# Layer 0 attention: the product of probabilities and values for two query tiles at once, in two-part reduced-precision operands

## The reference, cut to what matters

```
q = (h @ dequant(qw_q)).heads   # 32 heads; 4-bit weights with a scale per 128 rows
k, v = the same with 8 heads    # each serves 4 query heads (REP0 = 4)
q, k = rope(q), rope(k)
scores = q @ k.T / sqrt(128), causal
attn = softmax(scores)
ctx = attn @ v                  # <- the product that is changed
x = x + gate * (ctx @ dequant(qw_o))
```

## Time and profile before

| | |
|---|---|
| median of three runs | 1750.33 us |
| the profiled execution's own time | 1747.66 us |
| its span, first to last instruction | 1745.8 us |
| mean granted TensorE clock | 0.978 of 2.4 GHz |
| busy: PE, DVE, ACT, POOL | 1654.7, 1170.5, 1044.1, 747.5 us |
| first and last weight load of the changed product (L778) | 74.1 and 967.1 us |
| from an output product of head 0 to the same one of head 30 | 102.6 to 939.8 us, 30 heads |

### The profile page before, as it was taken

How to read it: one execution, slowest core, us unless ns; L and a number is a source line. 1 busy time by engine, 2 the same in 40 slices (tenths; PEclk the granted TensorE clock), 3 DMA queues, 4 the chain that set the end, 5 groups by cost and what they waited for, 6 DMA issues and landing times. The chain is left out here.

```text
span 1745.8 us, 28527 instructions
## 1 busy us (share of the span) xinstructions
PE 1654.7 (95%) x10107; PEld 1337.1 (77%) x10123; DVE 1170.5 (67%) x2951; ACT 1044.1 (60%) x2261; POOL 747.5 (43%) x705
## 2 busy tenths in 40 slices
PE   4899999999999999999999799999988999999897
PEld 2699989999999989899988488878764555555476
DVE  5767677777777676777666743336777777776285
ACT  3477777877777777777777221114324666666553
POOL 3286585675856757567551300000352334321200
PEclk9999999999999999999999889999979999999998
DMA  6100000101010010000000512200230000000000
GB/s 195 38 14 24 26 25 20 31 13 38 13 31 25 19 37 13 25 19 25 13 19 7 166 46 70 68 1 19 84 83 13 1 1 1 1 1 1 1 19 31
DMA packets 75014, 55.82 MB, mean 32 GB/s; under 512 B 23502, under 2 KB 57998, under 8 KB 74874
## 3 DMA queue, kind: packets, MB, share of 16 engines
q1 hardware_dynamic: 73290, 53.21, 10.5%
q10 hardware_dynamic: 1584, 0.79, 0.2%
HBM read 51.88 MB, written 2.10 MB: 31 GB/s over the span
## 5 line engine op out<-in xcount | busy, mean ns | idle before, releaser
L778 PEld LDWEIGHTS psum<-a_probsT,a_v 128*128 128x128 f32 x2304 | 294.7, 191 | 25.6 <-issue 3.9
L778 PE MATMUL psum<-a_probsT,a_v 128*128 128x128 f32 x2304 | 299.2, 275 | 1.7 <-ACT a_probsT L988 1.6
L877 DVE CUSTOM_DVE_ANT_0 psum<-psum,a_keys_allowed 128x128 f32<-128x128 f32 (+7 forms) x256 | 195.7, 764 | 83.1 <-PE psum L78 74.5
L2109 ACT ACTIVATE a_probsT<-psum 128x512 f32<-128x512 f32 (+1 forms) x304 | 168.4, 588 | 106.1 <-PE psum L1976 67.4
L971 ACT ACTIVATE a_probs<-psum,a_neg_max 128x128 f32<-128x128 f32 (+7 forms) x256 | 190.7, 745 | 66.4 <-DVE a_neg_max L877 58.0
L980 ACT ACTIVATE a_probs<-a_probs,a_row_inv 128x128 f32<-128x128 f32 (+7 forms) x256 | 201.2, 786 | 27.8 <-DVE a_row_inv L884 27.6
L641 POOL TENSOR_TENSOR a_turned_pool<-a_q_sum,a_sine 64x512 f32<-64x512 f32 x62 | 79.3, 1279 | 286.8 <-DVE a_q_sum L863 285.6
L907 DVE TENSOR_TENSOR a_ctxT_lo<-psum,a_ctxT_hi 128x128 fp32r<-128x128 f32 x256 | 73.5, 287 | 172.7 <-ACT a_ctxT_hi L994 172.6
L988 ACT COPY a_probsT<-psum 128x512 f32<-128x512 f32 (+3 forms) x384 | 173.3, 488 | 18.8 <-PE psum L766 16.6
L897 DVE SCALAR_TENSOR_TENSOR a_sumT<-psum,a_scale_o,a_sumT 128x512 f32<-128x512 f32 x248 | 173.5, 741 | 0.9 <-PE psum L792 0.8
L766 PE MATMUL psum<-ident,a_probs 128*128 128x128 f32 x1152 | 168.9, 274 | 0.5 <-ACT a_vT L965 0.3
(11 more groups left out here) (394 smaller groups left out, 3891.3 us busy)
## 6 DMA issues: line engine op xcount, KB each, us to landing
a_raw_o<-in_L_attn_qw_o SPq DMA_DIRECT2D x32, 256.0 KB, 2.8
a_raw_q<-in_L_attn_qw_q SPq DMA_DIRECT2D x31, 256.0 KB, 3.6
mod1b_w<-in_L_wmod SPq DMA_DIRECT2D x4, 1024.0 KB, 6.2
mod0a_w<-in_L_wmod SPq DMA_DIRECT2D x3, 1024.0 KB, 12.8
mod0b_w<-in_L_wmod SPq DMA_DIRECT2D x3, 1024.0 KB, 7.5
f_raw<-in_L_ffn_down_w SPq DMA_DIRECT2D x10, 256.0 KB, 3.1
f_raw<-in_L_ffn_gate_w SPq DMA_DIRECT2D x10, 256.0 KB, 3.3
f_raw<-in_L_ffn_up_w SPq DMA_DIRECT2D x10, 256.0 KB, 3.6
```

Of the source, the lines that this page charges most:

```text
L778: last = nc.tensor.matmul(bank(use)[:, 0:P], v[:, g % 2, j, :], probsT[:, u % 2, j, :], start=(j == 0), stop=(j == i))
L877: nc.vector.tensor_tensor_reduce(out=scores, in0=scores, in1=keys_allowed[:, S - (i + 1) * P:S], scale=-1.0, scalar=-MASKED, op0=ALU.add, ...
L2109: nc.scalar.activation(probsT[:, s % SLOTS, hs[0]:hs[-1] + 1, first:HALF], scores_of(group, n, HALF - first), ACT.Exp).then_inc(exped.sem, 1)
```

## The change

The product of probabilities and v is done once for two query tiles (2m and 2m + 1 of a head) with 256 columns, and with both operands in two f32r parts: three products for each of the 2m + 1 key tiles that both query tiles see. The last key tile, which only the odd query tile sees, keeps one float32 product with 128 columns (`own`). `values` for the pair stands in every odd iteration, at the place where one of a single unit stood in every iteration.

The operands have to be made: ACT copies the turned probabilities to `probsT_hi` (and the last key tile of an odd unit to `own` by a copy of its own), and DVE, new, computes `probsT_lo` from the bank and `probsT_hi` (`low_probs`) at the end of its iteration. The bank of turned probabilities is free only after DVE's part, not after ACT's. The values get the same parts (`high_v` on ACT, two instructions in `take_v` on DVE), at iterations 2 and 4 of a group's first head, in place of iteration 25 of the group before and 1.

What moves besides: outputs are one in each iteration in place of two in each odd one; `invert(u + 1)` stands behind the additions of iteration u in place of ahead of them in iteration u + 1; the last quarter of each q half is scaled out by ACT to a tile `extra` (`take_extra`) and added by POOL, in place of one addition on DVE; `split_values` and `high_values` work on 256 columns once for two units. The raw integers of k and v share one buffer, and SP's loads stand in another order for that; some tiles lie inside `sumT`.

The core of the diff:

```diff
 def outputs_due(h, p):
-    return [(h - 1, p - 1), (h - 1, p)] if h > 0 and p % 2 else []
+    return [(h - 1, p)] if h > 0 else []
 def v_turn(h, p):
     g, w = h // REP0, h % REP0 * NT + p
-    if w == 25 and g < LAST_GROUP:
-        return g + 1, 0
-    if w == 1 and g > 0:
-        return g, 1
+    if w in (2, 4) and g > 0:
+        return g, 0 if w == 2 else 1
+def pair_due(u):
+    if u % 2 == 0 or u < 3:
+        return []
+    h, i = units[u - 3]
+    return [(h, i // 2)]
 # the ring of banks
-        uses.append(("pv", *units[u - 2]))
+    uses += [("pv", *pair) for pair in pair_due(u)]
+by_act_too = lambda key, k: k == KT - 1 and key[0] == "q" and key[1] > 1
 # rope, on POOL for these
+if key in extras:
+    engine.wait_ge(*extra_out.of(key))
+    compute.tensor_tensor(x, x, extra[:, :], ALU.add).then_inc(counter.sem, 1)
+    engine.wait_ge(*counter.of((key, "extra")))
 # taken_out, what PE waits for before it uses a bank again
     if kind == "t":
-        return turned_out.of(name)
+        return lowered.of(name)
+    if key in extras and k == KT - 1:
+        return extra_out.of(key)
 # PE
-def values(u):
+def values(h, m):
-    pe.wait_ge(*turned_out.of(pieces_of(h, i)[-1]))
-    for j in range(i + 1):
-        last = nc.tensor.matmul(bank(use)[:, 0:P], v[:, g % 2, j, :], probsT[:, u % 2, j, :],
-                                start=(j == 0), stop=(j == i))
+    pe.wait_ge(*lowered.of(pieces_of(h, 2 * m + 1)[-1]))
+    for j in range(2 * m + 1):
+        split_products(nc.tensor, bank(use)[:, 0:2 * P], [part[:, j, :] for part in v_parts],
+                       [part[:, j, :] for part in probsT], j == 0, False)
+    nc.tensor.matmul(bank(use)[:, P:2 * P], v[:, 2 * m + 1, :], own[:, :], start=False, stop=True
+                     ).then_inc(filled.sem, 1)
 # DVE
+def low_probs(u):
+    h, i = units[u]
+    for piece in pieces_of(h, i):
+        first_key = piece[2] * TPH
+        keys = slice(first_key, min(first_key + TPH, i + 1 - i % 2))
+        turned = bank(("t", *piece))[:, 0:(keys.stop - keys.start) * P].rearrange("p (j q) -> p j q", q=P)
+        dve.wait_ge(*turned_out.of(piece))
+        nc.vector.tensor_tensor(probsT[1][:, keys, tile(i % 2)], turned,
+                                probsT[0][:, keys, tile(i % 2)].bitcast(F32), ALU.subtract).then_inc(lowered.sem, 1)
 # DVE's loop over the units
-    invert(u)
     if u + 1 < len(units):
         maximum(u + 1)
 ...
-        if k:
+        if k and not by_act_too(key, k):
             add_partial(key, k)
 ...
-    if u > 1:
-        split_values(*units[u - 2])
+    if u + 1 < len(units):
+        invert(u + 1)
+    for due in pair_due(u):
+        split_values(*due)
+    if u > 0:
+        low_probs(u - 1)
 # ACT
 def take_turned(u):
 ...
+        if i % 2 and keys.stop == i + 1:
+            keys = slice(first_key, i)
+            nc.scalar.copy(own[:, :], bank(use)[:, tile(i - first_key)])
+        turned = bank(use)[:, 0:(keys.stop - first_key) * P].rearrange("p (j q) -> p j q", q=P)
+        nc.scalar.copy(probsT[0][:, keys, tile(i % 2)], turned).then_inc(turned_out.sem, 1)
```

More of the change, by code:

```diff
@@ L458, in layer0_attention_phase @@
     firsts = [use[1] for use in uses if use[0] == "part" and use[2] == 0]
-    added_partials = [partial for partial in partials if partial[1]]
+    by_act_too = lambda key, k: k == KT - 1 and key[0] == "q" and key[1] > 1
+    extras = [key for key, k in partials if by_act_too(key, k)]
+    added_partials = [partial for partial in partials if partial[1] and not by_act_too(*partial)]
     pool_ropes = []
@@ L501, in layer0_attention_phase @@
         summed, ctx_lo, v_taken = count("summed", added_partials), count("ctx_lo", all_values), count("v_taken", v_turns)
+        lowered = count("lowered", pieces)
         ROPE_STEPS = ("sine", "cosine", "sum", "hi", "lo")
-        pool_roped = count("pool_roped", [(key, step) for key in pool_ropes for step in ROPE_STEPS])
+        pool_roped = count("pool_roped", [(key, step) for key in pool_ropes for step in ("extra",) * (key in extras) + ROPE_STEPS])
         dve_roped = count("dve_roped", [(key, step) for key in dve_ropes for step in ROPE_STEPS])
@@ L576, in first_weights @@
         def first_weights(act):
-            for n, (raw, arrived, made) in enumerate(((raw_q, q_in, wq_made), (raw_k, k_in, wk_made), (raw_v, v_in, wv_made))):
+            for n, (raw, arrived, made) in enumerate(((raw_q, q_in, wq_made), (raw_kv, k_in, wk_made), (raw_v0, v_in, wv_made))):
                 act.wait_ge(arrived, 32)
@@ L665, in _ @@
                     load_o(sp, h + 1)
-                if h % REP0 == 0 and g < LAST_GROUP:
-                    load_kv(sp, "v", g + 1)
         @block.gpsimd
@@ L790, in output @@
                 w = wo[:, h % 2, tile(j)]
-                nc.tensor.matmul(bank(use)[:, :], w, ctxT[1][:, h % 2, half(b)], start=True, stop=False)
-                nc.tensor.matmul(bank(use)[:, :], w, ctxT[0][:, h % 2, half(b)], start=False, stop=True).then_inc(filled.sem, 1)
+                nc.tensor.matmul(bank(use)[:, :], w, ctxT[1][:, (2 * h + b) % 3, :], start=True, stop=False)
+                nc.tensor.matmul(bank(use)[:, :], w, ctxT[0][:, (2 * h + b) % 3, :], start=False, stop=True).then_inc(filled.sem, 1)
             def turn_scale_o():
@@ L846, in _ @@
                 output(LAST_HEAD, n)
-            values(len(units) - 1)
+            values(*LAST_PAIR)
             for t in first_half:
@@ L1016, in _ @@
                         take_first(use[1])
+                    elif use[0] == "vt":
+                        high_v(*use[1:])
                     elif use[0] == "so":
@@ L1023, in _ @@
                         take_first(key)
-                if u > 1:
-                    high_values(*units[u - 2])
+                    elif by_act_too(key, k):
+                        take_extra(key)
+                if v_turn(h, p):
+                    high_v(*v_turn(h, p))
+                for due in pair_due(u):
+                    high_values(*due)
                 if u > 0:
```

111 lines of the change are left out of this document (66 added, 45 removed).

## The result

The changed kernel takes 1850.65 us (median of 4 runs, 1849.53 to 1852.53) against 1751.32 us (1746.1 to 1756.56, 4 runs): a ratio of 1.0568, 95% interval 1.0534 to 1.0602. It is slower by 99 us, where the prediction said 74, and stands 0.65 us beyond the end of its range. The profiled execution took 1851.61 us, its span 1849.8. First part one of the page, to set against the earlier trace rows.

The account below looks back on a forecast made before the run. The prediction took PE to bound the kernel before, at 27.91 us a head, and expected waits to outweigh its 1.40 us saving: 1747.7 + 63 (steady heads) + 11 (v turns) = 1822 us, range 1735 to 1850.

Parts of the forecast that it names:

- the walk: One head's eight iterations stepped through with slots and handovers: steady head 30.0 us against 27.91, +63 us over 30 heads; chance 0.57.
- Rival A: Steady heads: the waits don't come, since all engines have room; 1703 us, -45 us; chance 0.20.
- Rival B: Steady heads: only the two waits for q quarters come, +0.3 us a head, about 1763 us; chance 0.15.
- Rival D: New product's slot is 0.15, not 0.12 us: +25 us on the forecast; 0.05 shared with the longer-ring case.
- Rival C: v turns push the whole next iteration or handovers are longer: 1850 us and over; 0.05 shared with the longer-slot case.
- the steady head is 30.0 us: 26.6 of work on PE and 3.4 of waits: Period of a head in the changed phase: against 27.91, +2.1 us a head, +63 us over 30 heads.
- the ring: Closed chain across DVE, ACT and PE: maximum, exponential, first quarters, copies, lo part, next maximum; sets five of eight iterations.
- I take 0.08 from DVE to PE: Assumed handover from the end of DVE's slot to PE's start, 0.08 us.
- The prediction's bound for longer links: If each of 25 or so links in a head is 0.05 us longer: +1.2 us a head, +100 us.
- The v term: A group's first head: DVE's added instructions behind v turns, 2.4 us less 0.8; seven times 1.6 is +11 us.
- The last group, the first head and the tail I cost at nothing: Ends of the phase: no cost, since without k and v quarters the chain gets shorter by about 1.9 us.

Follow-up runs that it names:

- e2: Changed kernel with ACT taking the first quarters of q, k and v out of their banks ahead of the iteration's exponential: 1808.02 us, ratio 1.0317 to the kernel before.
- e10: Changed kernel with DVE's lo parts for 8 of 128 columns behind the first head, and first quarters ahead of ACT's exponential: 1755.32 us, ratio 1.0017.
- e5: Kernel before with one output product in each iteration and `invert` moved behind the additions: 1779.38 us, ratio 1.0162.
- e11: Changed kernel with the output products again two in each odd iteration: 1866.12 us, ratio 1.067 to the kernel before.
- e4: Changed kernel with DVE's lo part of the probabilities made for 8 of each 128 columns, but in the first head: 1781.18 us, ratio 1.0171 to the kernel before.
- e14: Kernel before with only `invert` moved behind the additions of the iteration: 1749.97 us, ratio 0.9991.

## Why the prediction was right or wrong

**Right: the sign and the mechanism.** PE's waits came in the five iterations where the walk had them, and one more of 0.18 us in p = 4. e2 and e10 show that they and the lo parts are the cost, and e2 came out as the walk gave it. The 30 heads from 101.03 to 1029.65 took 928.6 us, where the prediction said about 910. Rival A (no waits, 1703) is out: PE stands still 45 us in 600, by the records alone. Rival B (only the two waits for q quarters) is out: with both gone, e2 is still 57 us slower than before. Rival D is out by the spacing of 0.12 us (544.80 to 544.92), and e10's steady head of 27.33 us leaves no room for 1.4 us more of product on 26.6. Rival C, a walk whose ring is a little longer, at 1850 us and over, is where the time fell: it had 0.05. POOL's added instructions held up nothing: no wait of PE is ended by POOL in these lists.

**The size: 104 us of span in place of 74.** From the starts of heads 1, 28 and 31, the end of the phase and the span, in us of both kernels:

| part | before, after | longer by | predicted | missed |
|---|---|---|---|---|
| up to head 1 | 95.08, 101.03 | 5.95 | 0 | 6 |
| 27 heads to head 28, six with v turns | 852.74, 940.22 | 81.5 | 57 + 10 | 15 |
| three heads to the last, one with v turns | 933.02, 1029.65 | 9.15 | 6.3 + 1.6 | 1 |
| last head and tail | 976.68, 1076.80 | 3.5 | 0 | 3.5 |
| behind the phase | 1745.8, 1849.8 | 3.9 | 0 | 4 |

The first failing step, with 15 of the 30 us missed, is the term "the steady head is 30.0 us: 26.6 of work on PE and 3.4 of waits". It is 30.53, and by PE's own rows what was too small in it is the work. The walk against the timeline of one head (the scores' first instruction in each iteration, p = 0 at 538.92 for 0 to 4, the head before it for the rest):

| p | 0 | 1 | 2 | 3 | 4 | 5 | 6 | 7 | next 0 |
|---|---|---|---|---|---|---|---|---|---|
| walk | 0 | 3.60 | 8.22 | 10.54 | 13.36 | 16.28 | 21.20 | 25.25 | 29.9 |
| trace | 0 | 3.76 | 8.53 | 10.83 | 13.69 | 16.85 | 21.75 | 25.69 | 30.53 |

Iterations 2, 3 and 5 fit within 0.04 us. The walk is short in p = 0 by 0.16, since it was entered with DVE 0.17 us too early (1.47; the maximum stands at 540.56, 1.64 behind PE's start, as the walk itself found for the next head), in p = 1, 4 and 7 by 0.15 to 0.24, and in p = 6 it is long by 0.11.

Add up the distances from start to start on PE in that head (508.39 to 538.92). The gaps in which PE waits come to 3.4 us, the walk's own figure, though in part by luck: 1.8 in p = 5 to 7 in place of 2.3, but 0.4 in p = 1 in place of 0.2, and 0.2 in p = 4 in place of none. So the work is 27.1 us, not 26.6. A steady head of the kernel before, which has no such gaps, less the product's 1.40 gives 26.45; the other 0.7 us stands in the instructions that end a gap. Eight of them have a slot 0.07 to 0.11 us longer than usual. After, in p = 5, a slot of 0.34 us and then the usual 0.23:

```profile
527.08 0.51 PE L740 MATMUL psum<-hT_lo,a_wq 128*128 128x512 f32 x1 [0.37 <-ACT a_q_sum L1002]
527.42 0.39 PE L741 MATMUL psum<-hT_hi,a_wq 128*128 128x512 f32 x1
527.65 0.39 PE L812 MATMUL psum<-a_ctxT_lo,a_wo 128*128 128x512 f32 x1
```

The kernel before has the same behind the wait in its last head whose first row is in the earlier trace rows, 0.34 and then 0.23:

```profile
957.81 0.40 PE L792 MATMUL psum<-a_ctxT_hi,a_wo 128*128 128x512 f32 x1
958.04 1.53 PE L778 MATMUL psum<-a_probsT,a_v 128*128 128x128 f32 x12
```

The prediction took PE's work in a head with waits to be that of a head without any. In p = 1 and 7 these slots lie on the ring: the product takes 2.81 and 2.08 us there, the walk has 2.74 and 2.02.

Two handovers were short besides. "I take 0.08 from DVE to PE" had no row (the one from ACT to PE had none either, but the walk's 0.15 was near the 0.16 measured). DVE's last lo part leaves its slot at 544.38, the start of the next maximum, and the product starts at 544.61, 0.23 us later (5.26 to 5.38, 0.12, in the walk). And 0.13 from DVE's maximum to ACT's exponential is one row's, that of six key tiles; with eight it is 0.18, in the prediction's own rows (513.78 in the earlier trace rows to 513.96 in the earlier trace rows) and after (533.08 to 533.26). How the 0.53 us divides between these handovers and the longer slots, no run separates. The prediction's bound for longer links (0.05 in each of 25: +1.2 us a head) was wide enough for them; its range was not.

The v term was right: a head with v turns is 2.48 us longer than its neighbours, 2.4 worked out. The 1.6 us net of it is in the 81.5 six times and in the 9.15 once. Its 0.8 for the turns before measured 0.96 (twice 28.33 less 27.85), and 27.91, the mean of 30 heads, held them already, along with the shorter heads at the end. From 27.85 to 30.53 a steady head is 2.68 us longer, where the prediction has 2.1.

The second failing step is "The last group, the first head and the tail I cost at nothing". It measured 5.95 us up to head 1, 3.5 in the last head and tail and 3.9 behind the phase. In the first head (60 to 101 us) PE waits 9.2 us in all, 8.7 of them for DVE's new work, in place of 7.0 before:

```profile
PE psum L76 <- DVE a_probsT_lo L940: 4.0, 1, 4.0
PE psum L760 <- DVE a_v_lo L891: 3.5, 1, 3.5
PE psum L787 <- DVE a_v_lo L891: 1.2, 1, 1.2
```

In the last head PE waits up to 2.66 us for a lo part:

```profile
1057.24 0.36 PE L76 MATMUL psum<-a_probsT_hi,a_v_lo 128*128 128x256 f32 x1 [2.66 <-DVE a_probsT_lo L940]
```

The earlier trace rows had shown 0.82 and 0.86 us of such waits in the last head of the kernel before, and I used them as a sign of thin cover only and not for a price. Which share of the 5.95 us is the two differences for v and which the lo parts, no run separates. Of the 3.5 us, 0.8 lies behind the start of the last transposes and goes with the granted clock (see the last section). Of the 3.9 us behind the phase, where the code is the same, nothing shows a cause; the runs of one kernel lie up to 10 us apart.

**Not priced: the order of the outputs.** The walk had it inside (it used the new uses of the banks), so no term of the sum is wrong by it. But the prediction spoke of the added work and its ring only. By e5 one line of `outputs_due` costs the kernel before 29 us, more than a quarter of the whole loss; by e11 the changed kernel would not get them back from it.

**Two rules that the prediction cited.** The Trainium skill, in "Perfetto Trace Analysis", section "Identifying the Most-Contended Engine", would have the most-contended engine improved first. PE was lightened (9595 records for 10107, slots of 0.12 for 0.22 us) and the time rose all the same, so the trace speaks against the rule here. The Trainium skill, in "TensorEngine Tiling (Array Packing)", section "PSUM Bottleneck", says of another way to cheaper products that the emptying of PSUM may become the limit. The trace agrees: e4 leaves PE's work as it is and makes only DVE's differences out of PSUM smaller, for 69.5 us.

## What to carry to other kernels

Where three engines hand banks round, walk through one period with the handovers in it: here busy sums of 92, 77 and 73% of PE, DVE and ACT hid a loss of 5.7%, and the walk found its place and some seven tenths of its size. Take no handover without a row, let the instruction behind each gap cost more than its slot without one, and price the first and last period apart: in both, PE's longest waits for a lo part were 4.0 and 2.66 us there, against 0.4 in the steady heads. Before giving DVE work that reads a bank, look at what ACT has behind its next wait: moving the first quarters ahead of the exponential was worth 43 us, about what the product was to save (45).

## What the runs showed of the hardware

A handover has no single length for a pair of engines. From the end of a slot to the start of what waited for it: from DVE's lo part of the probabilities to PE 0.22 to 0.23 us (544.38 to 544.61), but from its lo part of ctx, in the kernel before, 0.14 (957.33 to 957.47):

```profile
957.12 0.29 DVE L907 TENSOR_TENSOR a_ctxT_lo<-psum,a_ctxT_hi 128x128 fp32r<-128x128 f32 x1 [1.43 <-ACT a_ctxT_hi L994]
957.33 0.15 DVE L884 RECIPROCAL a_row_inv<-a_row_sum 128x1 f32<-128x1 f32 x1
```

From PE to DVE it was 0.20, from ACT to PE 0.16 (542.11 to 542.27), from DVE's maximum to ACT 0.13 and 0.18 (above). And a wait on PE costs more than its gap: the instruction that ends it has a slot 0.07 to 0.11 us longer (527.08 to 527.42 against 527.42 to 527.65).

At the end of the phase the same 16 transposes take 1.97 us in the kernel before and 3.27 in the one after. PE in both, behind the same wait:

```profile
973.17 1.97 PE L809 MATMUL psum<-ident,a_sumT 128*128 128x128 f32 x16 [1.91 <-DVE a_sumT L897]
```

```profile
1072.47 3.27 PE L830 MATMUL psum<-ident,a_sumT 128*128 128x128 f32 x16 [1.90 <-DVE a_sumT L919]
```

The granted clock in the last stretch, of before and of after:

```profile
971.00:976.68 5.68, 2.23 (x18) 1.73 (x16) 4.60 (x9) 0.03 (x1) 0.00 (x0) 1.00 0.00 0
```

```profile
1071.00:1076.80 5.80, 3.27 (x16) 2.88 (x16) 4.17 (x8) 0.03 (x1) 0.04 (x1) 0.71 0.00 0
```

After shows 0.71, a mean of 2.4 GHz and of 1.2 in the same stretch, where before stayed at 2.4. PE had stood still for 2.66 us ahead of 1057.24 and for 1.90 ahead of these transposes; before, for 1.91 ahead of them. So the same instructions, unchanged, can take 1.3 us more by the clock alone. That the waits of the phase bring the clock down is likely but not shown. The transposes took 1.97 us in e4, e5 and e10 and 2.81 to 3.63 in the versions with the whole lo part; but in e14, whose PE is as busy as before's just ahead of them (16.42 us against 16.41 of 18.10), they took 2.49:

```profile
973.39 2.49 PE L809 MATMUL psum<-ident,a_sumT 128*128 128x128 f32 x16 [1.91 <-DVE a_sumT L897]
```
